# Moving the transposes between the matmul tiles of a fused recurrent-attention and FFN kernel, with the ScalarE and VectorE lists that follow

## What is computed

```python
pre = layernorm(x) @ W + b                      # 256 -> 1024: i, f, o, z
i = 10 * tanh((i_pre + input_bias) / 10);  f = -softplus(f_pre)
m' = max(f + m, i)                              # along the sequence
c = exp(f + m - m') * c + exp(i - m') * tanh(z)
n = exp(f + m - m') * n + exp(i - m')
h = sigmoid(o) * c / (n + 1e-6)
x = x + h / sqrt(mean(h * h) + 1e-8) * scale
g = layernorm(layernorm(x))                     # with gamma, beta
x = x + layernorm(x) + 0.5 * (silu(g @ W1 + b1) @ W2 + b2)    # W1, W2 dequantised
```

## Time and profile before

| | |
|---|---|
| median of 3 runs | 321.74 us (321.66 to 321.97) |
| the profiled execution | 321.89 us, its span 320.0 us |
| PE busy | 303.9 us, 95% |
| DVE busy | 267.4 us, 84% |
| ACT busy | 229.7 us, 72% |
| POOL busy | 118.1 us, 37% |
| mean granted TensorE clock | 0.989 |

### The profile page before, as it was taken

The page is one execution under the profiler, slowest core; times in us unless marked ns, Lnnn a source line. Parts: engine busy times, 40 slices in busy tenths (PEclk is TensorE's granted clock), DMA queues, the critical chain, the costliest instruction groups (busy, mean ns, idle before and its releaser), DMA issues.

```text
span 320.0 us, 4813 instructions
## 1 busy us (share of the span) xinstructions
PE 303.9 (95%) x1760; PEld 263.8 (82%) x1760; DVE 267.4 (84%) x474; ACT 229.7 (72%) x372; POOL 118.1 (37%) x126
## 2 busy tenths in 40 slices
PE   0999999999899997999999999999999999999996
PEld 0787788887898877988899888988899899899896
DVE  3998999999999999998969987888959899863531
ACT  3598966999599938489694978779593876941930
POOL 2162035002483179015920187014991156154000
PEclk9999998999999999799999999999999999999999
DMA  7990000000000020020000200010000100100101
GB/s 274 357 374 14 1 0 2 0 0 0 2 1 2 33 98 3 34 98 2 1 2 33 98 0 2 33 36 0 1 2 25 43 0 0 68 0 5 63 0 68
DMA packets 10951, 14.21 MB, mean 44 GB/s; under 512 B 688, under 2 KB 10160, under 8 KB 10672
## 3 DMA queue, kind: packets, MB, share of 16 engines
q1 hardware_dynamic: 10512, 13.12, 11.8%
q10 hardware_dynamic: 416, 0.79, 0.7%
HBM read 9.71 MB, written 4.19 MB: 43 GB/s over the span
## 4 chain that ended last, share of the span: by engine, by line
PE 45%; DVE 20%; issue 14%; POOL 12%; ACT 6%; DMA 3%; POOLq 0%; DVEq 0%; SPq 0%
PE mm_ps L221 7%; PE mm_ps L219 7%; PE mm_ps L220 7%; PE z_ps L220 6%; PE z_ps L219 6%; PE z_ps L221 6%; POOL rows L1034 3%; DVE rec L672 2%; DVE g L729 2%; DMA rows<-x 2%; POOL rec L1001 2%; DVE rows L737 2%; POOL g L1019 2%; DVE bn L742 2%; DVE rec L687 2%
## 5 line engine op out<-in xcount | busy, mean ns | idle before, releaser
L219 PE MATMUL z_ps<-w_hi,y_hi 128*128 128x256 f32 x248 | 71.3, 288 | 1.4 <-issue 1.4
L220 PE MATMUL z_ps<-w_lo,y_hi 128*128 128x256 f32 x248 | 70.4, 284 | 0.0
L221 PE MATMUL z_ps<-w_hi,y_lo 128*128 128x256 f32 x248 | 70.4, 284 | 0.0
L765 DVE TENSOR_TENSOR y_lo<-y,y_hi 128x512 fp32r<-128x512 f32 x64 | 43.2, 687 | 12.2 <-ACT y_hi L504 11.7
L501 ACT ACTIVATE y<-mm_ps,b_all 128x512 f32<-128x512 f32 x60 | 41.3, 688 | 13.4 <-PE mm_ps L288 9.8
L219 PEld LDWEIGHTS z_ps<-w_hi,y_hi 128*128 128x128 f32 x248 | 47.5, 191 | 1.9 <-issue 1.8
L220 PEld LDWEIGHTS z_ps<-w_lo,y_hi 128*128 128x128 f32 x248 | 47.2, 190 | 0.1
L221 PEld LDWEIGHTS z_ps<-w_hi,y_lo 128*128 128x128 f32 x248 | 47.1, 190 | 0.0
L1005 POOL TENSOR_TENSOR rrms<-meansq,minus_half 128x4 f32<-128x4 f32 x8 | 9.0, 1122 | 96.5 <-DVE meansq L723 96.5
L219 PE MATMUL mm_ps<-gt_hi,w_hi 128*128 128x512 f32 x108 | 43.2, 400 | 0.0
L220 PE MATMUL mm_ps<-gt_lo,w_hi 128*128 128x512 f32 x108 | 42.8, 396 | 0.0
(11 more groups left out here) (154 smaller groups left out, 669.4 us busy)
## 6 DMA issues: line engine op xcount, KB each, us to landing
out<-rows SPq DMA_DIRECT2D x15, 256.0 KB, 2.1
rows<-x SPq DMA_DIRECT2D x7, 512.0 KB, 6.4
q<-fc_q SPq DMA_DIRECT2D x2, 1024.0 KB, 12.1
s<-fc_scales SPq DMA_DIRECT2D x1, 1024.0 KB, 11.2
wg_raw<-fc_scales SPq DMA_DIRECT2D x1, 1024.0 KB, 11.1
wg_raw<-w_gates SPq DMA_DIRECT2D x1, 512.0 KB, 5.5
wg_raw<-w_gates ACTq DMA_DIRECT2D x1, 512.0 KB, 5.8
rows<-x ACTq DMA_DIRECT2D x1, 256.0 KB, 3.4
```

Of the source, the lines that this page charges most:

```text
L219: pe.matmul(dst, wh[w_at], ah[a_at], start=start, stop=False)
L220: pe.matmul(dst, wh[w_at], al[a_at], start=False, stop=False)
L221: return pe.matmul(dst, wl[w_at], ah[a_at], start=False, stop=stop)
L765: dve.tensor_tensor(y_lo[:, j], y[:, j % YBUFS], y_hi[:, j].bitcast(F32), ALU.subtract).then_inc(y_lo_done, 1)
```

## The change

On PE, in the stages t = 4 to 6, two of the four fc2 tiles are put in front of `g_turned` and the other two between `g_turned` and `x_turned`; two of the eight fc1 tiles are put between `x_turned` and `h_turned`. On ACT, `g_high` goes behind `reciprocal` and `exp_i`, the load of the silu table in front of `x_high`, and two silu tiles in front of `square_sums`. On DVE, `g_low` goes from in front of `base_bias` to behind `final(t-3, 0)`, `h` in front of that `final`, `x_low` behind `maximum`, and the `y_low` tiles begin earlier between the other steps. No operation is added or taken away; POOL's and SP's lists, and the stages before and behind these three, stay as they are.

```diff
--- before.py
+++ after.py
@@ -397,12 +397,13 @@
             fc1(1, range(5, KF))
             for t in range(4, CHUNKS - 1):
                 gates(t, range(GJ))
+                fc2(t - 3, range(0, 2))
                 g_turned(t - 2)
-                fc2(t - 3, range(0, 2))
+                fc2(t - 3, range(2, TT))
                 x_turned(t + 1)
-                fc2(t - 3, range(2, TT))
+                fc1(t - 2, range(0, 2))
                 h_turned(t - 1)
-                fc1(t - 2, range(KF))
+                fc1(t - 2, range(2, KF))
             gates(7, range(GJ))
             g_turned(5)
             fc2(4, range(TT))
@@ -574,14 +575,15 @@
                 gates(t, range(0, 7))
                 x_normalised(t + 1)
                 gates(t, range(7, GJ))
-                g_high(t - 2)
                 act.preload_act_table_set("natural_log_exp_and_others")
                 reciprocal(t - 1)
                 exp_i(t)
+                g_high(t - 2)
+                act.preload_act_table_set("silu_and_others")
                 x_high(t + 1)
-                act.preload_act_table_set("silu_and_others")
+                silu(t - 2, range(0, 2))
                 square_sums(t - 1)
-                silu(t - 2, range(KF))
+                silu(t - 2, range(2, KF))
                 act.preload_act_table_set("sigmoid_and_others")
             gates(7, range(GJ))
             act.preload_act_table_set("natural_log_exp_and_others")
@@ -906,26 +908,26 @@
                 divisor(t - 1)
                 numerators(t - 1)
                 o_times_c(t - 1)
-                g_low(t - 2)
                 base_bias(t - 3)
                 newton(t - 1)
                 refined(t - 1)
+                h(t - 1)
                 final(t - 3, 0)
-                h(t - 1)
-                x_low(t + 1)
+                g_low(t - 2)
                 input_times_z(t)
                 maximum(t, range(KD))
+                x_low(t + 1)
                 final(t - 3, 1)
+                y_low(t - 2, range(0, 2))
                 mean_square(t - 1)
-                y_low(t - 2, range(0, 1))
+                y_low(t - 2, range(2, 3))
                 h_scaled(t - 1)
-                y_low(t - 2, range(1, 2))
+                y_low(t - 2, range(3, 4))
                 residual(t - 1)
-                y_low(t - 2, range(2, 3))
+                y_low(t - 2, range(4, 5))
                 ln2_sums(t - 1)
-                y_low(t - 2, range(3, 4))
+                y_low(t - 2, range(5, 6))
                 ln2(t - 1)
-                y_low(t - 2, range(4, 6))
             y_low(4, range(6, KF))
             denominators(6, range(KD))
             divisor(6)
```

## The result

The changed kernel takes 324.50 us (median of 4 executions, 323.78 to 325.42) against 321.74; the ratio is 1.0086, 95% interval 1.0059 to 1.0114. It is slower, by 1.9 to 3.7 us. Its profiled execution took 323.78 us with a span of 321.8, 1.8 over the span before. Measured again later (e11) it had 325.15 against 322.03, ratio 1.0091 (1.0062 to 1.0120).

The account below looks back on a forecast made before the run. PE bounds steady stages; stage 4 has a 2.05 us PE pause for gt_lo and a slow clock behind it. Terms 0.9 + 0.5 + 0.9 = 2.3 us gave 324.1 us against 321.74, range 321.4 to 327.4.

Parts of the forecast that it names:

- The wait in front of x: Stage 4: PE waits 3.4 us for gt_lo before x_turned, where it waited 2.05, as g_low starts 6.8 us later.
- Stage 4, +0.9 us: Stage 4: the longer pause before x_turned makes stage 5 start at 148.90 against 147.96, 0.9 us later.
- the old 1.65 us for the clock: Stage 4: PE's lower clock behind the x pause costs 1.65 us, taken as unchanged from the kernel before.
- "No wait" for h: Stage 4: x_low's first half is there by 139.1, h_turned comes at some 139.5, so PE does not wait.
- Stages 5 and 6, +0.5 us: Late newton delays x_low; h_turned waits 0.4 us, a tenth more for the second half, in one of the two stages.
- Stage 7, +0.9 us: Stage 7: POOL starts 3.3 us later, so base(4) and base_bias come late and delay newton; 0.9 us reaches the end.
- My lower end of 0.2 us: Stage 7: newton is only 0.2 us late if POOL's tiles run free once DVE stands waiting for them.
- Sum against median: Whole kernel: terms add 2.3 us to the profiled 321.89, giving 324.2; the median lies 0.15 lower, at 324.1.
- Rival 1: Stages 5 and 6: POOL's list becomes the bound, x and h wait 2.4 us in one stage; 326 to 327.8; chance 0.18.
- Rival 2: Stage 4: the pause costs no clock, so the stage gives -0.7 us and the kernel takes 321.0; chance 0.11.
- Rival 3: Only stage 4 counts, h and the base keep their slack; 322.5 to 322.9 us; chance 0.14.
- rival 4: Whole kernel: no difference, within 0.64 us; slow stretch half as dear, with a small loss later; chance 0.12.

Follow-up runs that it names:

- e11: The changed kernel measured once more, with nothing altered, against the kernel before; 325.15 us against 322.03, ratio 1.0091.
- e9: Changed kernel with, in stage 4 alone, g_low right behind o_times_c on DVE and g_high in front of reciprocal on ACT; 325.42 us, ratio 1.0095.
- e4: Changed kernel with 16 matmuls that nobody reads filling PE's pause before the x transposes of stage 4; 323.96 us, ratio 1.0072.
- e3: Changed kernel with POOL's base(4) moved from stage 7 to behind base(3) in stage 6; 324.86 us, ratio 1.0103.
- e6: Kernel before, with its old lists on PE, ACT and DVE, and POOL's base steps one chunk earlier; 321.55 us, ratio 0.9986.
- e10: Changed kernel with, in stage 4 alone, g_low behind o_times_c, x_low behind h, and g_high in front of reciprocal; 321.38 us, ratio 0.9972.
- e2: Changed kernel's new lists in stages 5 and 6 alone, stage 4 with the lists of the kernel before; 322.82 us, ratio 1.0033.
- e1: Changed kernel's new lists in stage 4 alone, stages 5 and 6 with the lists of the kernel before; 324.33 us, ratio 1.0087.
- e5: Changed kernel with POOL's base steps one chunk earlier, so that DVE need not wait at base_bias; 323.33 us, ratio 1.0043.

## Why the prediction was right, and where it was not

The forecast was 324.1 us, 0.7% slower; the time is 324.50. The sum was +2.3 us on the profiled execution, and from G4 on it is +2.2. That the two are so close is luck in part: stage 4 cost 0.4 us more than I had, stages 5 and 6 cost 0.5 less, and the two cancel. The terms:

- **The wait in front of x, 3.4 us against 2.05.** It is 3.90, and `x_turned` starts at G4 + 27.68 where the prediction had 134.35 - 106.91 = 27.44. The chain was the one forecast: `base_bias` waits 1.45 us for POOL, `g_low` starts 5.4 us behind `base_bias` (5.3 forecast). PE was ready 0.3 us earlier than I had it. e9 shows that `g_low`'s place, with that of `g_high` it needs, is the cause of this wait, and that moving it alone only hands the wait to h.
- **Stage 4, +0.9 us.** It is +1.3. Of the 0.4 us, 0.24 lie in the later start of x and 0.16 behind it. What I had wrong behind it is the make-up, not the size: I took the old 1.65 us for the clock and "No wait" for h. From x to h stage 4 took 1.71 us over the bare work, but e4, with the clock at 1.00, still took 1.05 over it, most of it waits for `xt_lo` (0.72) and the second half of `gt_lo` (the x transposes take 0.98 us in place of 0.79). The two causes lie over each other, so that neither alone gives back more than its difference.
- **Stages 5 and 6, +0.5 us.** Nothing. I had `newton` at T + 17.9 because `x_normalised` would wait for POOL's `ln1_root`. POOL's g tiles took 3.21 us, and `ln1_root` was in time; `newton` ran at 166.15 - 148.89 = T + 17.3, held by `base_bias`, and `x_low` started at T + 26.3, in time for h at T + 27.3.
- **Stage 7, +0.9 us.** +0.87, and e3 confirms the cause: the g tiles took 7.04 us beside the scans, `base(4)` came late, and ran at 2.17 us for four tiles once DVE stood still. `newton` came 1.0 us late. Two sizes were off in opposite directions: I had 5.64 for the g tiles and 3.22, or somewhat less, for `base(4)`. My lower end of 0.2 us for this term does not follow from its own figures: 1.3 less the 0.55 between 3.22 and 2.67 is 0.75. And four `y_low` tiles, not three, stood between ln2 and the next stage in the old list (219.99 and 222.77 in its stage 7); DVE enters stage 7 at T + 3.2 all the same.
- **Sum against median.** I set the median 0.15 us under the profiled execution, as before. It is 0.7 over it, and no step of the prediction has this. The profiled execution of the changed kernel is its shortest. A lower mean clock goes with only a part of the rest: one of the other three is at 0.984, but the longest, a span of 323.4 us, is at 0.989 like the profiled one. In which stage they lose it stays open, since only the profiled executions show stages.

Rival 1 (POOL bounds stages 5 and 6) did not come. POOL's shift was there and DVE waited 2.14 us at `base_bias`, but `gt_lo` was there 1.2 us before PE wanted it (170.40 + 0.88 against 172.52). The Trainium skill, SBUF — State Buffer, section Who interferes with whom, calls the port pair that the two engines share an exclusive lock, and has a DVE instruction with two SBUF inputs contend with a GpSimd instruction that reads SBUF. POOL's four tiles at 7.04 us beside scans and products against 2.17 beside an idle DVE agree with it. Rival 2 (no price in clock) did not come in any of the profiles with a pause of over 3 us in stage 4; behind a pause of 2.1 us it came once, in e6. Rival 3 fell with stage 7, and rival 4 with the interval of the ratio. The forecast saw some 4.1 us to win in stage 4, but it took DVE's list as part of the change and asked only what it costs; that the same order of TensorE gives 4.4 us there under another list of DVE is what e10 adds.

## What to carry to other kernels

When work is moved on the bounding engine to cover a late operand, list beside it what stands in front of that operand on its own engine, and put there only what the bounding engine waits for sooner. Here PE came to the x transposes 5.2 us later after G4, and `g_low` started 7.0 us later; the wait grew by the difference. The same TensorE order with `g_low` and `x_low` first in stage 4 alone was 0.3% under the kernel before in place of 0.9% over it (e10), and 1.1% under it (e7) with the earlier base steps on POOL and the same two steps moved forward in stage 5 as well. A step moved into the cover must be checked together with the next operand on the same engine (e9 against e10), and effects under the spread of executions are read from stage lengths, not from medians.

## What the runs showed of the hardware

A pause of TensorE of the same length has no fixed price. Behind the 2.1 to 2.2 us pause of stage 4 the clock fell in the profiles of the kernel before and of e2 (8.3 us from x to h) and stayed at 1.00 in e6 (6.8 us). With a pause of 3.9 to 4.0 us x to h took 5.40 us twice, 5.45 once (e3) and 6.13 once (e1), and with one of 3.2 us 6.28 (e5). In e1, e5 and e9 the clock fell while PE still stood, and it was low about twice as long as in the five profiles of stage 4 where it fell behind the pause. The mean granted clocks of executions come in steps (0.995, 0.989, 0.984, 0.979), and neighbouring steps of the kernel before lie some 1 to 1.5 us of span apart. In all 14 profiles the step follows from two places, the one near 52 us and stage 4: 0.994 or 0.995 is a short stretch at the first alone, 0.979 a long one at both. The Trainium skill, TensorE: Matmul & The Clock Gate, section Part 1: The HAM clock gate, gives the clock exactly two levels; the windows here read 1.00, 0.50 and mixtures of the two and agree with it.

POOL and DVE slow each other both ways: four tensor_scalar tiles of POOL (128x256) took 2.17 us with DVE idle and 7.04 beside its scans and products, and DVE's products took up to 1.47 us instead of 1.22 beside POOL's tiles in e5. One of the four there kept its 1.21.
